# Third block: mask products and maxima on VectorE in turns of two instead of turns of four

## The reference, cut to what matters

```python
def attention(q, k, v, mask):
    scores = jnp.einsum('bhqd,bhkd->bhqk', q, k) / jnp.sqrt(jnp.float32(HD))
    scores = scores * mask - 10000.0 * (1.0 - mask)
    probs = jax.nn.softmax(scores, axis=-1)
    return jnp.einsum('bhqk,bhkd->bhqd', probs, v)
ln_out = layernorm(hidden_states, ln1_s, ln1_b)
qkv = ln_out @ w_qkv + b_qkv
...
ctx = merge_heads(attention(split_heads(q), split_heads(k), split_heads(v), ltor_mask))
x = hidden_states + ctx @ w_ao + b_ao
...   # the same once more with ln2, keys and values of encoder_states, and cross_mask
mlp_out = gelu(ln_out @ w1 + b1) @ w2 + b2
return x + mlp_out
```

## Time and profile before

| | before |
|---|---|
| median of 3 runs | 1542.82 us |
| time of the profiled execution | 1538.59 us |
| its span | 1536.8 us |
| TensorE busy | 1467.4 us (95%) |
| VectorE busy | 914.9 us (60%) |
| ScalarE busy | 902.3 us (59%) |
| GpSimd busy | 140.9 us (9%) |

### The profile page before, as it was taken

How to read it: one execution, slowest core, us unless ns; L and a number is a source line. 1 busy time by engine, 2 the same in 40 slices (tenths; PEclk the granted TensorE clock), 3 DMA queues, 4 the chain that set the end, 5 groups by cost and what they waited for, 6 DMA issues and landing times.

```text
span 1536.8 us, 28652 instructions
## 1 busy us (share of the span) xinstructions
PE 1467.4 (95%) x9824; PEld 1131.2 (74%) x9824; DVE 914.9 (60%) x3306; ACT 902.3 (59%) x2807; POOL 140.9 (9%) x171
## 2 busy tenths in 40 slices
PE   7999999999999999999999999999899988999996
PEld 5766688878787878687878787778666666866664
DVE  4777722445454545545545545531999995178887
ACT  5878933434444434443444444433899997289996
POOL 2010011000000000100000000011222222022200
PEclk9999999999999999999999999999999999999999
DMA  7000103010010100101001000000100100000000
GB/s 295 2 2 1 39 26 124 1 41 23 1 63 1 48 16 1 64 0 49 15 1 64 1 1 0 1 0 1 56 2 9 36 15 8 1 1 9 22 2 15
DMA packets 10879, 40.66 MB, mean 26 GB/s; under 512 B 2416, under 2 KB 2672, under 8 KB 8688
## 3 DMA queue, kind: packets, MB, share of 16 engines
q1 hardware_dynamic: 10736, 38.82, 7.0%
HBM read 37.77 MB, written 1.05 MB: 25 GB/s over the span
## 4 chain that ended last, share of the span: by engine, by line
PE 66%; ACT 16%; DVE 4%; issue 3%; DVEq 0%; POOLq 0%; ACTq 0%; POOL 0%
ACT probs L980 10%; PE bank L809 7%; PE bank L790 7%; PE bank L823 7%; PE bank L782 7%; PE bank L769 7%; PE bank L772 7%; PE bank L749 5%; PE bank L738 5%; ACT pT L988 4%; PE bank L798 4%; PE bank L583 2%; PE bank L567 2%; DVE probs L1245 2%; DVE probs L1227 1%
## 5 line engine op out<-in xcount | busy, mean ns | idle before, releaser
L980 ACT ACTIVATE probs<-probs,negmax 128x256 f32<-128x256 f32 (+1 forms) x640 | 349.4, 559 | 44.1 <-DVE negmax L1245 43.6
L1061 ACT ACTIVATE pT<-bank 128x512 f32<-128x512 f32 x128 | 76.5, 597 | 387.8 <-PE bank L798 387.8
L583 PEld LDWEIGHTS bank<-ident,probs 128*128 128x128 f32 x1536 | 167.4, 141 | 120.6 <-ACT probs L980 61.8
L583 PE MATMUL bank<-ident,probs 128*128 128x128 f32 x1536 | 226.0, 280 | 30.8 <-ACT pT L988 19.8
L1390 DVE TENSOR_REDUCE stats<-bank 128x1 f32<-128x257 f32 x256 | 108.5, 425 | 212.1 <-PE bank L790 211.1
L1245 DVE CUSTOM_DVE_ANT_0 probs<-bank,mask_a 128x256 f32<-128x256 f32 (+1 forms) x384 | 174.1, 508 | 31.2 <-PE bank L567 26.5
L988 ACT ACTIVATE pT<-bank 128x512 f32<-128x512 f32 x288 | 171.2, 596 | 9.6 <-PE bank L583 9.5
L809 PE MATMUL bank<-pT,probs 128*128 128x256 f32 x512 | 132.7, 381 | 2.7 <-ACT pT L1061 2.7
L790 PE MATMUL bank<-kT,pT 128*128 128x257 f32 x512 | 132.7, 382 | 0.6 <-ACT pT L1044 0.6
L980 ACT ACTIVATION_READ_ACCUMULATOR probs<-probs,negmax 128x1 f32 x640 | 133.1, 208 | 0.0
L1052 ACT ACTIVATE probs<-bank,stats 128x257 f32<-128x257 f32 x256 | 118.7, 474 | 3.5 <-DVE stats L1393 3.5
(11 more groups left out here) (111 smaller groups left out, 2489.4 us busy)
## 6 DMA issues: line engine op xcount, KB each, us to landing
w_m<-in_w SPq DMA_DIRECT2D x6, 1024.0 KB, 7.4
g_qkv<-in_g SPq DMA_DIRECT2D x4, 1536.0 KB, 7.5
q_res<-in_g SPq DMA_DIRECT2D x4, 1536.0 KB, 6.8
w_qkv<-in_w SPq DMA_DIRECT2D x3, 768.0 KB, 4.4
g_bv<-in_gbv SPq DMA_DIRECT2D x8, 256.0 KB, 7.1
g_o<-in_go SPq DMA_DIRECT2D x4, 512.0 KB, 3.4
q_res<-in_go SPq DMA_DIRECT2D x4, 512.0 KB, 3.4
rows<-in_rows SPq DMA_DIRECT2D x1, 1664.0 KB, 14.1
```

The source lines that it names most:

```text
L583: last = nc.tensor.transpose(out[:, n * P:(n + 1) * P], probs[:, u % PROBS, q * T + t * P:q * T + (t + 1) * P], ident[:, :])
L980: last = nc.scalar.activation(s, s, ACT.Exp, bias=negmax[:, u % PROBS, k:k + 1], scale=-1.0, accum_out=sums[:, tile % 2, q, j * c.res + r: ...
```

## The change

The first loop of products takes two units instead of four, and in the main loop two products follow after every second maximum instead of four after every fourth. The number of products, of maxima and of every other instruction is the same, and no list other than VectorE's is changed.

```diff
                 if c.kinds == "mult":
-                    for u in range(QUAD):
+                    for u in range(QUAD // 2):
                         times_mask(u)
                     mlp_sums(1, B - 1)
                 for slot in range(c.last_slot() + 1):
                     if slot < c.count:
                         maxima(slot)
-                        if c.kinds == "mult" and slot % QUAD == 3 and slot + 1 < c.count:
-                            for u in range(slot + 1, slot + 1 + QUAD):
+                        if c.kinds == "mult" and slot % 2 == 1 and slot + 1 < c.count:
+                            for u in (slot + 1, slot + 2):
                                 times_mask(u)
```

## The result

| | before | after |
|---|---|---|
| median | 1540.89 us (4 runs) | 1554.15 us (4 runs) |
| lowest to highest | 1538.76 to 1542.89 us | 1553.64 to 1555.97 us |
| time of the profiled execution | 1538.59 us | 1555.97 us |
| its span | 1536.8 us | 1554.2 us |

The ratio of after to before is 1.0091, with a 95% interval of 1.0075 to 1.0108. Forecast were 1554 us and a loss of 12.5 us; the ratio says 14 us.

The account below looks back on a forecast made before the run. ScalarE was taken to set the pace, with VectorE tied to it once per part. First border 1.7, six others 9.9 and last quad 0.9 made 12.5 us: 1554 us, range 1545.5 to 1561.

Parts of the forecast that it names:

- The chain at the borders: Borders between parts: late last product delays scores, transposes and ScalarE's copy; 1.65 us at each of six borders, 9.9 us.
- Paid each time: VectorE's wait for the reciprocals gives back its lead, so every border costs again; rival of paying once: 1541 to 1545.5, chance 0.09.
- 13.53 + 0.2: VectorE's 13.53 us from the reciprocals' copy to the late product's end, plus 0.2 us until the scores start.
- 14 us for L1274: Sign in the changed trace: VectorE's wait for the reciprocals from TensorE's L625 grows from 3.7 to about 14 us.
- The start: Block's start: first exponential 1.2 us earlier, waited away at ScalarE's first copies; net 0, bounds -1.2 and 0.
- the first border: Scores of unit 16, after a part with no tie before it: 1.86 us late less 0.15 in hand, 1.7 us.
- The last quad: Block's end, no border following: scores 1.27 us late if VectorE has followed ScalarE's delay fully, 0 if not; taken as 0.9.
- The port: GpSimd's bias addition L1504 beside maxima, taken as 0; as rival 0.9 us in six places, 1556.5 to 1560.7, chance 0.09.
- maxima that stretch beside L1504: Sign in the changed trace that the forecast is wrong and the port rival holds.
- The rival: Port rival: bias additions hold maxima back 0.9 us in six places; 17.9 us in all, 1556.5 to 1560.7, chance 0.09.
- the two levels of the kernel before: Runs before lay near 1538.59 and 1542.82 us; adding 12.5 gives 1551.1 or 1555.3, and 1554 was said.
- Switching VectorE between products and maxima more often: VectorE's 32 additional turns: cost taken as 0, upper bound 2.9 us of lost overlap in all.

Follow-up runs that it names:

- e3: Changed kernel with GpSimd's bias additions L1504 in the block's loop cut to 4 of 256 columns (output not the reference's): 1550.00 us, ratio 1.0071.
- e2: Kernel before with only the last quad of each part split in two and two products: 1550.09 us, ratio 1.0074.
- e6: Kernel before with only the quad of units 76 to 79 split, so one border alone: one execution, 1540.91 us.
- e7: Kernel before with the products of units 0 to 7 in turns of two, all later ones in fours: one execution, 1539.87 us.
- e9: Kernel before with only each border's quad split, three products and then unit 15's alone behind the maximum of unit 13: one execution, 1550.64 us.
- e1: Changed kernel, but the last quad of each part keeps its four products in a row behind the third quad's last maximum: 1548.96 us, ratio 1.0052.
- e4: Kernel before with GpSimd's bias additions L1504 cut to 4 of 256 columns (output not the reference's): 1539.63 us, ratio 1.0001.
- e8: Kernel before with GpSimd's bias addition L1504 released two maxima earlier, meant to run beside maxima: 1538.86 us, ratio 0.9996.
- e10: Kernel before with GpSimd's bias addition L1504 released one maximum earlier, to start beside a quad's last maximum: one execution, 1544.70 us.

## Why the prediction was right, and where it wasn't

**The chain at the borders** was right in every link: last product behind the maximum of unit 13 and the values, scores 0.15 to 0.2 us behind it, transposes, ScalarE's copy. Priced at 1.65 us for six borders (9.9 us), it measured 9.4 us in e3 and in e2 (their steps summed, less those of before).

**Paid each time** was right (e2, e6), and the reason mostly. From the border's scores to VectorE's copy of the reciprocals it is 14.0 us in e2 (1211.72 to 1225.68) and 14.1 before, from that copy to the next border's scores 13.7 us (to 1239.37) instead of 12.0: the forecast had 13.53 + 0.2. VectorE does wait longer in each part, but the forecast put it all on the reciprocals and said 14 us for L1274; it was 7.7. The rest stands at the products of the part's second quad, whose scores TensorE reaches late behind the late border; in e2, with the order inside the part as before, the same wait is 0.76 us. The two waits of one part after:

```profile
1222.21 1.29 DVE L1227 TENSOR_TENSOR probs<-bank,mask_m 128x512 f32<-128x512 f32 x2 [0.77 <-PE bank L567]
...
1227.23 0.42 DVE L1274 COPY recipT<-bank 128x256 f32<-128x256 f32 x1 [1.15 <-PE bank L625]
```

I had overlooked the first of them; it holds VectorE as well, and the sum is about the same (7.7 + 5.6 = 13.3 us).

**The start** was said to be a net zero swallowed by the first border, 1.7 us together. By itself it costs 1.3 to 1.4 us (e7). Together, without L1504 and with the clock full in that stretch (e3), start and first border cost 23.31 - 21.08 = 2.2 us: indeed not the sum of both (1.4, and 1.8 for the border alone in e9), but 0.5 over the forecast.

**The last quad** was put at 0.9 us; without L1504 the scores of unit 124 were 0.3 us later against those of unit 112 (18.87 against 18.59 in e3), and 0.4 of that came back before the last exponential.

**The port** was the mis-sized term: taken as 0, it measured 3.5 us (0.0, 0.2, 0.2, 0.8, 0.8, 0.8 in the six parts, each the step after less that of e3, and 0.7 at the last quad). The forecast had named maxima that stretch beside L1504 as a sign that it is wrong, and they did. I had judged L1504 by L1556, beside which the maxima of the rows kept their pace. The two are not alike. The rival had the mechanism and a price of 5.4 us, since it gave each of six places 0.9 us; where L1498 does not go first, L1504 starts earlier and costs 0.2. The rule of the Trainium skill (SBUF — State Buffer, section "SBUF: two separate sides"), that GpSimd and an instruction of VectorE with two inputs in SBUF exclude each other, agrees with L1504: the maximum that meets it ends 0.28 us behind it (1203.45 and 1203.17), and in all seven places of this trace 0.27 to 0.29. By its words it holds for L1556 as well, which reads SBUF too, and there the traces bear it out only in part: in the rows of before L1556 held no maximum, in e1 one beside it took 0.82 us, but ended well before it (1139.80, L1556 at 1140.40).

**In sum**, by the two profiles the block is 225.27 - 209.47 = 15.8 us longer (first product to last exponential). In e3, which has neither the port's share nor a stretch at half clock in the block, it is 11.5 us longer: 2.2 at the start and first border, 9.4 in the steps, 0.3 at the last quad, less the 0.4 that came back. So the forecast's own terms were 1.0 us too much together; the port adds 3.5 and the clock 0.8. That 12.5 lies so near to the 14 of the ratio is thus in part luck, since the two errors offset each other, and so is the 1554 us, a point chosen between the two levels of the kernel before.

The profiled executions lie 17.4 us apart, the medians 13.3. What the executions differ by beyond the block, 1.6 us, fits the clock. In the profile after, TensorE's granted clock was at half, the 1.2 GHz level, for 3.4 us right behind its long wait for the products of unit 7, and in three more stretches of that length after the block; the profile before had one such stretch there, and both have one at their very end. The stretch in the block, in the window's row:

```profile
1089.00:1092.40 3.40, 3.40 (x23) 2.45 (x16) 3.40 (x17) 1.30 (x4) 0.65 (x1) 0.50 0.00 0
```

It isn't the change's own: the kernels of e4, e6, e8 and e10, which have the old order there, had such a stretch near the block's start too, and their scores of unit 16 came 21.87 to 21.94 us behind the first product instead of 21.08. So a stretch there costs 0.8 to 0.9 us, and the change's kernel lost as much (24.14 against 23.31 in e3). In e2, where the border is late anyway, it cost 0.1 us (23.03 against e9's 22.90). Whether the change makes it more frequent wasn't tried.

## What to carry to other kernels

Where a producer waits until a whole group of buffers is free, look only at the last instruction that frees the group, and sum what a new order puts before it; how evenly the others lie is worth nothing if the full engine never waited for them. Then look at what stands behind the waiting instruction on its engine, for that is who pays, and ask at which wait the lead is given back, for that decides whether it is paid once or in each round. And when instructions move, look at what ran beside them: an addition on GpSimd that was hidden beside one operation of VectorE can hold the next one back.

## What the runs showed of the hardware

- A half maximum on VectorE (two inputs in SBUF, 128 x 256) that met a GpSimd addition of two tensors (128 x 512, 1.28 us) took 0.59 to 1.49 us instead of 0.42, the longer the earlier it met it, and ended 0.27 to 0.29 us behind the addition in each of nine places (seven in the changed kernel, two in e10); products with one input in PSUM kept their usual time beside the same addition (1.28 us for two).
- The GpSimd operation of one tensor L1556 (1.57 us, twice in a row) left maxima at 0.42 us in most places. But in e1 one half maximum in five parts took 0.82 us beside it, in e2 one in six parts 0.65 us, and at the block's start one took 0.82 us in six kernels. It was itself 0.2 to 0.4 us longer at times (3.35 to 3.54 instead of 3.12 us for two). What makes the difference to L1504, the number of its inputs or something else, stays open.
- Switching VectorE between products and maxima more often cost nothing visible: from the first product's start to the next maximum's it took 1.20 us with two products and 2.39 with four, and from a half maximum to a product 0.34 us, as from one half to the next.
